# Sixteen-head attention in four transformer layers: 77-key jobs widened to 128 rows, their mask put in the exp's bias, and three extra matmuls in 38 jobs

## The reference, cut to what matters

```python
def _attn(q, k, v, mask):                 # layers 0 to 2, H = 16, HD = 8
    s = jnp.einsum('bqhd,bkhd->bhqk', q, k) * scale
    s = jnp.where(mask, s, jnp.finfo(s.dtype).min)
    a = jax.nn.softmax(s, axis=-1)
    return jnp.einsum('bhqk,bkhd->bqhd', a, v)
# attention 0: x on itself, 128 keys, a 128x128 mask     (layer 0)
# attention 1: x on the context, 77 keys, a mask (16,77) (layer 0)
# attention 2: x on the context, 77 keys, no mask        (layer 1)
# attention 3: x on itself, 128 keys, no mask            (layer 2)
# attention 4: x on the context, 77 keys, no mask        (layer 2)
```

## Time and profile before

| | |
|---|---|
| timed executions | 892.00, 904.67, 909.67 us; median 904.67 |
| profiled execution | 909.89 us, span 908.0 us |
| TensorE matmul busy | 764.2 us (84%), 9226 instructions |
| TensorE weight loads busy | 464.0 us (51%) |
| VectorE busy | 464.4 us (51%) |
| ScalarE busy | 356.9 us (39%) |
| GpSimd busy | 201.4 us (22%) |
| chain that ended last | PE 65%, ACT 17%, DVE 13%, issue 3% |

### The profile page before, as it was taken

One profiled execution on the slowest core, in us unless ns is written; L12 is line 12 of the kernel. 1 busy time (PEld: TensorE's weight loads), 2 busy tenths in 40 slices (PEclk: granted clock), 3 DMA queues, 4 the chain that ended last, 5 costly groups with the idle time before them and its releaser, 6 DMA issues.

```text
span 908.0 us, 21329 instructions
## 1 busy us (share of the span) xinstructions
PE 764.2 (84%) x9226; PEld 464.0 (51%) x9226; DVE 464.4 (51%) x1102; ACT 356.9 (39%) x570; POOL 201.4 (22%) x239
## 2 busy tenths in 40 slices
PE   5588888898789988788879888888899898887787
PEld 4245445354454555455545555564456654474455
DVE  3556766456734665546553564555645546133322
ACT  0032422443225342532424342524366533834543
POOL 1222324032310333213232321412321121000000
PEclk9989999798859996889966986988999969998999
DMA  8300000000000000000000000000000000000000
GB/s 315 105 1 14 2 13 14 1 14 12 14 1 2 13 14 14 2 1 25 2 13 1 13 13 2 3 13 1 13 1 1 13 2 2 1 1 12 0 1 24
DMA packets 15332, 16.13 MB, mean 18 GB/s; under 512 B 1833, under 2 KB 13108, under 8 KB 14856
## 3 DMA queue, kind: packets, MB, share of 16 engines
q1 hardware_dynamic: 14572, 10.72, 3.9%
q10 hardware_dynamic: 668, 4.05, 1.2%
HBM read 13.66 MB, written 1.09 MB: 16 GB/s over the span
## 4 chain that ended last, share of the span: by engine, by line
PE 65%; ACT 17%; DVE 13%; issue 3%; DMA 1%; POOL 0%; SPq 0%; POOLq 0%; DVEq 0%; ACTq 0%
PE avp L1019 17%; PE lin L902 13%; ACT P L547 10%; PE lin L915 10%; PE big L994 9%; PE big L970 3%; DVE xn L703 2%; DVE mhl L746 2%; PE big L1002 2%; PE lin L924 2%; DVE bst L690 2%; PE big L963 1%; PE big L987 1%; DVE oT L771 1%; PE big L990 1%
## 5 line engine op out<-in xcount | busy, mean ns | idle before, releaser
L547 ACT ACTIVATE P<-big 77x1024 f32<-77x1024 f32 (+1 forms) x160 | 154.7, 1018 | 309.4 <-PE big L1002 309.3
L746 DVE TENSOR_REDUCE mhl<-big 128x8 bf16<-128x616 f32 (+1 forms) x160 | 151.5, 963 | 111.1 <-PE big L970 110.4
L487 POOL TENSOR_TENSOR qm<-qT,hm 128x512 f32<-128x512 f32 x80 | 87.5, 1094 | 211.0 <-PE big L1002 110.9
L902 PE MATMUL lin<-hT,W 128*128 128x512 f32 x184 | 114.5, 712 | 12.3 <-ACT hid L581 5.8
L994 PE MATMUL big<-qm,kT 32*77 32x512 f32 (+1 forms) x640 | 106.8, 742 | 0.0
L1019 PE MATMUL avp<-P,Vp 77*32 77x128 f32 (+1 forms) x2560 | 103.6, 312 | 1.2 <-DVE Vp L713 1.2
L1019 PE MATMUL avp<-P,onesp 77*32 77x128 f32 (+1 forms) x2560 | 102.2, 310 | 0.0
L1019 PEld LDWEIGHTS avp<-P,Vp 77*32 77x32 f32 (+1 forms) x2560 | 76.4, 124 | 34.0 <-issue 28.7
L970 PE MATMUL big<-kbm,qb 32*128 32x308 bf16 (+1 forms) x320 | 55.9, 359 | 39.4 <-ACT P L547 38.7
L454 POOL TENSOR_SCALAR rstd<-mv 128x4 f32<-128x4 f32 (+1 forms) x36 | 8.4, 233 | 363.8 <-DVE mv L694 363.6
L1019 PEld LDWEIGHTS avp<-P,onesp 77*32 77x32 f32 (+1 forms) x2560 | 85.7, 127 | 2.4
(11 more groups left out here) (150 smaller groups left out, 875.8 us busy)
## 6 DMA issues: line engine op xcount, KB each, us to landing
gring<-gate_rows SPq DMA_DIRECT2D x20, 256.0 KB, 3.3
W<-in_w ACTq DMA_DIRECT2D x2, 1152.0 KB, 12.1
hid<-in_ws SPq DMA_DIRECT2D x2, 832.0 KB, 5.7
W<-in_w ACTq DMA_DIRECT2D x1, 1088.0 KB, 7.5
x<-in_x SPq DMA_DIRECT2D x4, 256.0 KB, 9.2
out<-x SPq DMA_DIRECT2D x4, 256.0 KB, 2.3
ctx<-in_ctx SPq DMA_DIRECT2D x4, 154.0 KB
ctxT<-in_ctxT SPq DMA_DIRECT2D x4, 154.0 KB
```

The source lines that it names most:

```text
L487: nc.gpsimd.tensor_tensor(qm[:, j % 2], q.broadcast_to([128, 4, T]), mask.broadcast_to([128, 4, T]), ALU.mult).then_inc(qm_ready, 1)
L547: nc.scalar.activation(P[0:kw, 8 * half:8 * half + 8, :], big[0:kw, 2 * half:2 * half + 2, :].rearrange("p g (h q) -> p (g h) q", h=4), AC ...
L746: v.tensor_reduce(mhl[:].rearrange("p (g c) -> p g c", c=32)[:, 2 * half:2 * half + 2, 0:4], big[:, 2 * half:2 * half + 2, 0:4 * kw].rearr ...
L902: i = mm(lin_ap(st, s, job, m)[:, 0:n], w, a, start=(c == 0), stop=(c == len(parts) - 1))
```

## The change

It has five parts.

- In jobs of 77 keys the second score computation now fills 128 rows: the slice of `kT` is 128 columns wide (it reaches past the batch's 77 keys into whatever lies behind), the subtraction's weights have 128 columns, the exp runs over 128 partitions, and `av` reads 128 rows of `P`, `Vp` and `onesp`.
- The exp of those jobs gets a bias with one value per partition: `padcol` (0 for keys, a large negative number for rows 77 to 127, so that these become 0) for a = 2 and 4, and `maskcol` (the mask and the padding) for a = 1. The four mask matmuls L990 of each of the 16 jobs of a = 1 are gone.
- The two columns are made at the start: 16 small matmuls into `big` ahead of `mods_done`, and a few small VectorE operations. `mcb` grows by 128 columns.
- The subtraction goes over the four 32-row groups inside each head instead of two and two, with the same 16 matmuls; `st_full` for the first half now comes with its 14th.
- `keep_warm(3)`: three bf16 matmuls of 128 rows, 128 columns and 512 elements into `mtp`, seen as 512 fp32 values. Nobody reads them. They stand behind the subtraction of the jobs in `IDLE`, the jobs that have no unit of TensorE between slots 0 and 1: 38 jobs (by attention 0 to 4: 8, 9, 10, 6 and 5).

```diff
+IDLE = [j for j in range(JOBS) if not any(slot == 4 * j and u[1] not in ("stat", "apply") for slot, u, s in PLACED)]
...
-        mtp = ps("mtp", [128, 1024], BF16)
+        mtpf = ps("mtp", [128, 512])
+        mtp = mtpf[:].bitcast(BF16)
...
             def exps(j, half):
-                kw = ATT[job_of(j)[0]]["kw"]
+                a, s, b = job_of(j)
                 act.wait_ge(st_full, job_turn(j, half, 2))
-                nc.scalar.activation(P[0:kw, 8 * half:8 * half + 8, :],
-                                     big[0:kw, 2 * half:2 * half + 2, :].rearrange("p g (h q) -> p (g h) q", h=4),
-                                     ACT.Exp, scale=float(HD) ** -0.5).then_inc(st_free, 1)
+                hidden = {} if ATT[a]["kw"] == T else {
+                    "bias": maskcol[:, s * GB + b:s * GB + b + 1] if a == 1 else padcol[:]}
+                nc.scalar.activation(P[:, 8 * half:8 * half + 8, :],
+                                     big[:, 2 * half:2 * half + 2, :].rearrange("p g (h q) -> p (g h) q", h=4),
+                                     ACT.Exp, scale=SCALE, **hidden).then_inc(st_free, 1)
...
+            chain(v.tensor_reduce(padcol[:], ident[:, C:128], AX, ALU.add))
+            v.tensor_scalar(padcol[:], padcol[:], -4.0 * BIG, None, ALU.mult).then_inc(mask_in, 1)
+
             dve.wait_ge(mods_done, 1)
+            v.tensor_scalar(maskcol[:], big[:, 3, 0:B], SCALE, padcol[:], ALU.mult, ALU.add)
...
+            pe.wait_ge(mask_in, 1)
+            for b in range(B):
+                i = mm(big[:, 3, b:b + 1], mcb[:, b * C:b * C + 128], oneb[:, 0:1], start=True, stop=True)
             i.then_inc(mods_done, 1)
...
                 pe.wait_ge(m_ready, job_turn(j, 1, 2))
-                for g in range(4):
-                    o = big[0:kw, g, :].rearrange("p (h q) -> p h q", h=4)
-                    if a == 0:
-                        mm(o, identb[:], mkq[:].unsqueeze(1).broadcast_to([128, 4, T]), start=True, stop=False,
-                           skip_group_check=True)
-                    elif a == 1:
-                        mm(big[0:kw, g, :], mcb[:, (s * GB + b) * C:(s * GB + b + 1) * C], oneb[:], start=True, stop=False, skip_group_check=True)
+                if a == 0:
+                    for g in range(4):
+                        mm(big[:, g, :].rearrange("p (h q) -> p h q", h=4), identb[:],
+                           mkq[:].unsqueeze(1).broadcast_to([128, 4, T]), start=True, stop=False, skip_group_check=True)
                 pe.wait_ge(qm_ready, job_turn(j))
                 for g in range(4):
                     r = slice(32 * g, 32 * g + 32)
-                    mm(big[0:kw, g, :].rearrange("p (h q) -> p h q", h=4), kT[s][r, b * kw:(b + 1) * kw],
-                       qm[r, j % 2], start=(a > 1), stop=False, skip_group_check=True)
+                    mm(big[:, g, :].rearrange("p (h q) -> p h q", h=4), kT[s][r, b * kw:b * kw + 128],
+                       qm[r, j % 2], start=(a > 0), stop=False, skip_group_check=True)
 
                 pe.wait_ge(mt_ready, job_turn(j))
-                for half in range(2):
-                    for hh in range(4):
-                        for g in (2 * half, 2 * half + 1):
-                            r = slice(32 * g, 32 * g + 32)
-                            i = mm(big[0:kw, g, hh * T:(hh + 1) * T], indb[r, hh, 0:kw], mT[r], start=False,
-                                   stop=(hh == 3), skip_group_check=True)
-                    i.then_inc(st_full, 1)
+                for hh in range(4):
+                    for g in range(4):
+                        r = slice(32 * g, 32 * g + 32)
+                        i = mm(big[:, g, hh * T:(hh + 1) * T], indb[r, hh, :], mT[r], start=False, stop=(hh == 3),
+                               skip_group_check=True)
+                        if hh == 3 and g % 2 == 1:
+                            i.then_inc(st_full, 1)
+
+            def keep_warm(n):
+
+                for _ in range(n):
+                    mm(mtpf[:], identb[:], oneb[:], start=True, stop=True)
...
-                        w = Vp[s][0:kw, b, 4 * g + hh, :] if part == 0 else onesp[0:kw, hh, :]
-                        i = mm(avp[32 * g:32 * g + 32, part * T:(part + 1) * T], w,
-                               P[0:kw, 4 * g + hh, :], start=(hh == 0), stop=(hh == 3), skip_group_check=True)
+                        w = Vp[s][:, b, 4 * g + hh, :] if part == 0 else onesp[:, hh, :]
+                        i = mm(avp[32 * g:32 * g + 32, part * T:(part + 1) * T], w, P[:, 4 * g + hh, :],
+                               start=(hh == 0), stop=(hh == 3), skip_group_check=True)
...
                         scores_t(u)
+                        if u in IDLE:
+                            keep_warm(3)
```

More of the change, by code:

```diff
@@ L36 @@
 BIG = 2.0 ** 100
+SCALE = float(HD) ** -0.5
 S_PARTS = [("ada0", 9), ("ssq", 2), ("sskv", 2), ("ada2", 6), ("e1a", 6), ("g1a", 1)]
@@ L279, in build @@
         mkq = sb("mkq", [128, T], BF16)
-        mcb = sb("mcb", [128, B * C], BF16)
+        mcb = sb("mcb", [128, B * C + 128], BF16)
+        padcol = sb("padcol", [128, 1])
+        maskcol = sb("maskcol", [128, B])
         mhalf = sb("mhalf", [128, GB])
@@ L337, in build @@
         mods_done, modv_done, tab_done = sem("mods_done"), sem("modv_done"), sem("tab_done")
+        mask_in = sem("mask_in")
         gates_mm, grow_done = sem("gates_mm"), sem("grow_done")
@@ L636, in _ @@
             v.tensor_scalar(indb[:], sel4[:].unsqueeze(2).broadcast_to([128, 4, 128]), -1.0, None, ALU.mult)
-            for dst, src in ((mqk, mqk8), (mkq, mkq8), (mcb[0:1], mc8)):
+            for dst, src in ((mqk, mqk8), (mkq, mkq8), (mcb[0:1, 0:B * C], mc8)):
                 v.tensor_scalar(dst[:], src[:], -1.0, BIG, ALU.add, ALU.mult)
+            chain(v.tensor_reduce(padcol[:], ident[:, C:128], AX, ALU.add))
+            v.tensor_scalar(padcol[:], padcol[:], -4.0 * BIG, None, ALU.mult).then_inc(mask_in, 1)
             dve.wait_ge(mods_done, 1)
+            v.tensor_scalar(maskcol[:], big[:, 3, 0:B], SCALE, padcol[:], ALU.mult, ALU.add)
             chain(v.tensor_tensor(modv[:], big[:, 0, 0:21 * B].rearrange("p (c b) -> p c b", b=B),
@@ L993, in scores_t @@
                     r = slice(32 * g, 32 * g + 32)
-                    mm(big[0:kw, g, :].rearrange("p (h q) -> p h q", h=4), kT[s][r, b * kw:(b + 1) * kw],
-                       qm[r, j % 2], start=(a > 1), stop=False, skip_group_check=True)
+                    mm(big[:, g, :].rearrange("p (h q) -> p h q", h=4), kT[s][r, b * kw:b * kw + 128],
+                       qm[r, j % 2], start=(a > 0), stop=False, skip_group_check=True)
                 pe.wait_ge(mt_ready, job_turn(j))
-                for half in range(2):
-                    for hh in range(4):
-                        for g in (2 * half, 2 * half + 1):
-                            r = slice(32 * g, 32 * g + 32)
-                            i = mm(big[0:kw, g, hh * T:(hh + 1) * T], indb[r, hh, 0:kw], mT[r], start=False,
-                                   stop=(hh == 3), skip_group_check=True)
-                    i.then_inc(st_full, 1)
+                for hh in range(4):
[8 more added lines that the diff above has]
+                    mm(mtpf[:], identb[:], oneb[:], start=True, stop=True)
             def av(j, part):
                 a, s, b = job_of(j)
-                kw = ATT[a]["kw"]
                 if part == 0:
```

## The result

| | median us | runs | profiled run | span | mean clock |
|---|---|---|---|---|---|
| before, same chip | 906.93 | 892.0 to 909.67 | 909.9 | 908.0 | 0.885 |
| after | 843.3 | 841.38 to 846.69 | 842.97 | 841.2 | 0.969 |

The kernel is faster: by the medians 64 us, 7.0%. The forecast was 870 and 846 to 891. The ratio applied to the 904.67 from which the forecast started gives 850, just inside it.

What follows compares the result with a forecast made beforehand. The prediction took TensorE, partly at half clock, to bound the kernel. Its terms, -36 -13 +6.5 +2 +1 +2 = -37.5 us from 909.9, gave 872; allowing for the timed median of 904.67 it predicted 870 us, range 846 to 891.

Steps and rivals of the forecast that it cites:

- The bound: TensorE over the whole kernel: 209 us of 908 at half clock, above all in 77-row jobs with nothing else for TensorE.
- The clock term: TensorE's mean clock rises from 0.885 to 0.94: 105 us less half clock at 0.34 each, gain 36 us.
- The mask matmuls: Attention 1's 16 jobs each get 0.83 us shorter without their four mask matmuls: gain 13 us, bounds 8 to 14.
- The bias column: The exp of 77-key jobs takes 88 ns more with a bias column: loss 6.5 us, bounds 0 to 8.6.
- The 128-column loads: Wider fp32 score loads in 48 jobs cost 0.04 us each, subtraction's loads nothing: loss 2 us, 4 at most.
- The extra matmuls: Three per job in 38 jobs fit TensorE's idle time before the next scores: loss 1 us, 4 if sticking out.
- The subtraction's order: First half's semaphore comes with the 14th matmul instead of the 8th: 0 us, otherwise 14 us over 80 jobs.
- The start: Sixteen small matmuls and `maskcol` ahead of the release delay the first norm: loss 2 us.
- Rival 2: Rows do not matter for the clock, only the extra matmuls help: 891 to 905 us, chance 0.17.
- Rival 3: Clock full nearly everywhere, 0.98 or more: 843 us, range 832 to 848, chance 0.14.
- Rival 4: Slower: attention 1 falls to half clock without its mask matmuls, loss 29 us, 937 us in all, chance 0.03.
- Rival 5: Later first half, protruding extra matmuls and slower exp all count while the clock gives nothing: about 923 us at most, chance 0.02.

Runs made afterwards that it cites:

- e4: Kernel before with attention 1's mask moved into the exp's bias over 77 rows, its 64 mask matmuls gone; 901.93 us, ratio 0.9977.
- e2: Kernel before with only the three extra 128-row matmuls in the 38 jobs; 853.75 us, ratio 0.9384.
- e5: Kernel before with only `av` of the 77-key jobs read over 128 rows, for time alone; 873.89 us, ratio 0.9623.
- e3: Kernel before with three extra matmuls of the same length in the 38 jobs, filling 32 rows instead of 128; 884.24 us, ratio 0.9746.
- e9: Kernel after with attention 1's four mask matmuls per job put back and its mask out of the bias column; 852.52 us, ratio 0.9522.
- e10: Kernel after with second scores and subtraction of 77-key jobs back at 77 columns; 842.58 us, ratio 0.9416.
- e6: Kernel before with only second scores, subtraction and attention 1's mask matmuls 128 columns wide; 901.31 us, ratio 1.0017.
- e8: Kernel before with the three extra matmuls and attention 1's mask in the exp's bias, all at 77 rows; 856.69 us, ratio 0.9542.

## Why the prediction was right, and by how much not

**The bound.** Right: the time was in the half clock, and the jobs of 77 rows with nothing beside them had it. Widening or filling them, each alone, took 44 and 55 us off.

**The clock term**, put at -36, is the step that failed in size. It was a product of two factors, and both were too small.
The first is the clock itself: I took 0.94, "near the middle of 0.87 and 1.00", and it is 0.969. I had read 0.82 of attention 3 as what widening could reach and 0.87 to 1.00 as what the extra matmuls could, and took the middle of the latter for the whole kernel; but the two add up. By widening alone attention 2 came to 0.89, with the extra matmuls to 0.94 to 1.00. Half-clock time fell by 157 us in the profiled runs (144 in the means), not by 105.
The second is the price, 0.34 us for each us at half clock, from one light job. Two readings exist. From run to run of one kernel the span changes by 0.345 us for each us of half clock (all kernels' timed runs together; before alone 0.35); e4's one run of 1181.49 us, nearly all at half clock, gives 0.33 against e4's others. Between kernels that changed little but the clock it is more: e2 (902.6 - 850.8) / (196 - 68) = 0.40, e5 32.6 / 86 = 0.38, e3 19.8 / 48 = 0.41 (against before on their own chips alone 0.39 to 0.40 each). With 0.40 the means close: 144 x 0.40 = 58 from the clock, and -58 - 11.4 (below) + 7 + 1 = -61.4, where 902.6 - 841.9 = 60.7 was measured; with 0.345 the same sum is -53. That the sum closes at 0.40 is a weak test, since the price was picked from kernels of this same set. A job with another unit beside it has more TensorE work under the same exp, so it should lose more than the light jobs 43 and 55; that explanation is argued and not measured, and which of the two prices holds for which jobs stays open.

**The mask matmuls**, put at -13 (8 to 14). e9 against after is 9.2 us by medians; corrected with 0.345 to equal half-clock time, the mean spans (851.2 with 46, 841.9 with 52) are 11.4 apart. Against e10, which ran on the same chip as e9 (841.6 with 53), it is 11.9. The step is right within its bounds. In job 43 the removal is 1.03 - 0.16 = 0.87, as worked out.

**The bias column**, put at +6.5. 90 to 94 ns an exp were measured where 88 were taken, and 0.15 us a job, so 7 us for 48 jobs. Right. Job 43 shows the two steps together: 5.7 without mask matmuls, plus 0.15, is the 5.85 of the row.

**The 128-column loads**, put at +2: too small to be seen. e6, which has them, is 1.8 us under before, and e10, which lacks them, 0.7 us under after, both within the scatter. **The extra matmuls**, put at +1: the next scores did not come later in jobs 43 and 55, and the wait in front of them is 0.53, where about 0.6 was forecast. **The subtraction's order**: 0, as far as the rows of job 43 show, where the exp starts 0.43 us behind the subtraction's start and 0.42 before the change; it had no run of its own. **The start**, put at +2: 0.4. I had priced each of the 16 matmuls by a 128-column load or the transpose; with one column they took 0.57 together.

**The rivals.** Rival 2 (rows don't matter) is out by e3 and e5. Rival 3's time (832 to 848) came, but not by its condition: the clock is 0.969, not 0.98 or more, and the larger price did the rest. Rival 4 is real as a mechanism and small: in e8 the loss of clock took most of the 11 us that the removed matmuls give, and e4's trace has 0.73 in four jobs that had 1.00, but neither made a clear loss of them. In the changed kernel widening and extra matmuls cover it. Rival 5 has nothing in the rows for it.

**The range.** Its low end, 846, was the top of case 3 "but not its core". The whole of what the clock could give, 71 us by the light job's price, was one end; with 0.40 it would have been 84, and 0.94 as "the middle" had no row of its own.

## What to carry to other kernels

Read the granted clock by stretch, and where it is low while TensorE looks busy, look at how many rows its matmuls fill: padding the contraction of `av` from 77 to 128 rows added no matmul and gave 29 us. A known wait of TensorE, whose length a row shows, can be filled with full-row matmuls that nobody reads; count their length against the wait, since beyond it they stick out (three gave 55 us alone, beside the widening five gave no measurable more than three). Ask of each matmul that is taken away whether it was also what kept the clock up: the removal of 64 of them gave nothing measurable in the kernel before, and 9 to 12 us once other matmuls kept the clock up.

## What was not expected of the hardware

- Matmuls of equal number and length (35.2 and 34.7 us in all) gave a mean clock of 0.962 with 128 rows and 0.918 with 32, and 30 us between them. `av` over 128 rows instead of 77 gave 0.932 against 0.885 with no matmul more.
- 51 more weight columns in the matmuls of 32 rows (and in the mask matmuls) did nothing that could be measured, neither for the clock (0.878) nor for the time (901.31 against 903.13).
- A matmul of one column and 128 rows is cheap in a row of 16: 0.57 us in all for the matmuls and 0.70 for their loads, which run beside them: some 45 ns each.
- The price of half clock is 0.345 us per us between runs of one program and 0.38 to 0.41 between programs.
- One trace lacked 38 of 114 matmul records of one line, the first of the three in jobs 43 and 55, and none of their loads. TensorE's busy time in such a trace is too small where they stood.
